# Hybrid edge passes of a four-layer GNN kernel: more strips and fewer gathered groups, the bias written into PSUM by ScalarE, two banks for expanded rows

## What is computed

```python
for l in range(5):
    h = leaky(x @ W1[l] + b1[l]) @ W2[l] + b2[l]                     # per node
    e = leaky(edge_attr @ We1[l] + be1[l]) @ We2[l] + be2[l]         # per edge, 32 -> 64 -> 64
    msg = h[src] * e * dot_scale[l]
    agg = segment_sum(msg, dst)
    out = x + agg * res_w[l]
    x = layer_norm(out) * ln_g[l] + ln_b[l]
```

## Time and profile before

| what | value |
|---|---|
| median of 3 runs | 14754.5 us (14753.59 to 14761.05) |
| the profiled execution, its own time | 14765.12 us |
| its span | 14763.1 us |
| PE busy | 11299.0 us, 77% of the span |
| POOL busy | 9919.2 us, 67% |
| DVE busy | 9782.0 us, 66% |
| ACT busy | 5832.6 us, 40% |
| mean granted TensorE clock | 0.860 of full speed |
| five hybrid passes, from their first gather to their last | 7346.8 to 13751.9 us |

### The profile page before, as it was taken

The page is one execution under the profiler, slowest core; times in us unless marked ns, Lnnn a source line. Parts: engine busy times, 40 slices in busy tenths (PEclk is TensorE's granted clock), DMA queues, the critical chain, the costliest instruction groups (busy, mean ns, idle before and its releaser), DMA issues. The chain is left out here.

```text
span 14763.1 us, 394431 instructions
## 1 busy us (share of the span) xinstructions
PE 11299.0 (77%) x124067; PEld 10168.6 (69%) x124067; DVE 9782.0 (66%) x18585; ACT 5832.6 (40%) x11169; POOL 9919.2 (67%) x10022
## 2 busy tenths in 40 slices
PE   0366666689566787878699979979997998899585
PEld 0244444588555787878588868868886887888485
DVE  8777777567798323232477777777777777777524
ACT  0000000122266555555355445544444554455354
POOL 0377777677496675757377767767776776777474
PEclk9877777555567999999899989999998999999798
DMA  3122222222177565656444434434443443444363
GB/s 115 33 56 56 56 56 56 56 78 80 58 247 252 186 201 161 201 166 198 112 130 131 120 91 131 131 78 134 131 127 86 131 130 86 129 131 130 107 203 116
DMA packets 1281251, 1800.75 MB, mean 122 GB/s; under 512 B 558054, under 2 KB 817510, under 8 KB 1279974
## 3 DMA queue, kind: packets, MB, share of 16 engines
q1 hardware_dynamic: 978113, 1423.30, 30.6%
q0 software_dynamic: 296960, 327.11, 10.0%
q10 hardware_dynamic: 5040, 35.13, 0.6%
HBM read 1475.83 MB, written 308.76 MB: 121 GB/s over the span
## 5 line engine op out<-in xcount | busy, mean ns | idle before, releaser
L1181 POOL DMA_INDIRECT rows_buf<-feature_table,idx_buf x4320 | 4529.1, 1048 | 1388.4 <-issue 1101.2
L881 POOL DMA_INDIRECT rows_buf<-feature_parts,idx_buf x2176 | 2058.9, 946 | 944.2 <-issue 362.8
L920 ACT ACTIVATE sums_space<-banks 128x384 bf16<-128x384 f32 x3920 | 1661.5, 450 | 1268.3 <-PE banks L937 1245.3
L937 PE MATMUL banks<-table_parts,tmp 128*128 128x192 bf16 x13720 | 1786.0, 247 | 372.9 <-DMA tmp<-one_hots 372.3
L735 POOL DMA_INDIRECT rows_buf<-attention_table,idx_buf x1664 | 1574.8, 946 | 554.2 <-issue 554.2
L1271 PE MATMUL banks<-attr_buf,params 128*128 128x256 f32 x5660 | 1587.6, 404 | 300.1 <-DMA attr_buf<-cell_attr 167.3
L950 PE MATMUL banks<-sums_space,tmp 128*128 128x192 bf16 x13720 | 1781.7, 247 | 0.0
L1233 ACT ACTIVATE sums_space<-onehot 128x448 bf16<-128x448 f32 (+1 forms) x1415 | 845.1, 597 | 2361.6 <-DVE onehot L1369 995.9
L1283 PEld LDWEIGHTS banks<-params,hidden 128*128 128x128 f32 x11320 | 1519.5, 195 | 195.1 <-issue 8.2
L1283 PE MATMUL banks<-params,hidden 128*128 128x128 f32 x11320 | 1521.7, 278 | 0.0
L937 PEld LDWEIGHTS banks<-table_parts,tmp 128*128 128x128 fp8e4 x13720 | 1196.0, 98 | 398.8 <-issue 396.5
(11 more groups left out here) (395 smaller groups left out, 20166.5 us busy)
## 6 DMA issues: line engine op xcount, KB each, us to landing
tmp<-one_hots SPq DMA_DIRECT2D x1855, 448.0 KB
attr_buf<-cell_attr SPq DMA_DIRECT2D x875, 128.0 KB
one_hots<-tmp SPq DMA_DIRECT2D x245, 448.0 KB
attr_buf<-attr SPq DMA_DIRECT2D x653, 128.0 KB, 2.2
rows_buf<-feature_table,idx_buf POOLq DMA_INDIRECT x4320
gathered_rows<-rows_buf SPq DMA_DIRECT2D x208, 272.0 KB, 2.1
rows_buf<-gathered_rows SPq DMA_DIRECT2D x208, 272.0 KB
rows_buf<-feature_parts,idx_buf POOLq DMA_INDIRECT x2176
```

The source lines that it names most:

```text
L881: pool.indirect_dma_start(out=far_rows[:, u, t, :], out_offset=None, in_=table3, in_offset=bass.IndirectOffsetOnAxis(ap=idx_buf[:, u, t:t ...
L920: act.activation(cell_rows[:, q, 0:width], bank[q][:, 0:width], ACT.Copy).then_inc(s_cells_sb, 1)
L937: ins = pe.matmul(bank[q][:, j % 2 * 3 * D:(j % 2 + 1) * 3 * D], src_cells[:, k, j, side * P:(side + 1) * P], table_parts[:, 2 * (k * CELL ...
L1181: pool.indirect_dma_start(out=edge_rows[:, u, t, :], out_offset=None, in_=table, in_offset=bass.IndirectOffsetOnAxis(ap=idx_buf[:, u, t:t ...
```

## The change

The split becomes 29 strips (203 near works) and 92 gathered groups: 295 works. The cycle is now 4 strips and 12 groups, 40 works, run 6 times, with a tail of 5 strips and 20 groups, 55 works. In the cycle each strip goes 0 F 1 2 F 3 4 F 5 6; in the tail the first goes 0 F 1 2 F 3 F 4 5 F 6, the other four 0 F 1 F 2 3 F 4 5 F 6.

ScalarE writes be2, repeated over 8 tiles, into the edge bank (`put_bias`, 128x512 f32), between `high_part` and `copy_hidden` in its turn; the bias product on PE and `split_bias` go. The expanded rows alternate between banks 0 and 7. Where a near work has no own edges (k of 2 and more), the last fp32 product of the second edge layer covers 64 columns rather than 128.

```diff
-        self.cell_strips, self.cell_rest, self.cell_turn = 25, 3, 8
-        self.cell_turns = (self.cell_strips - self.cell_rest) // 2
+        self.cell_strips, self.cell_cycle, self.cell_rest, self.cell_turn = 29, 4, 5, 12
+        self.cell_turns = (self.cell_strips - self.cell_rest) // self.cell_cycle
...
-        CYCLE, REST = mixed(2, L.cell_turn), mixed(L.cell_rest, L.cell_rest_far)
+        CYCLE, REST = mixed(L.cell_cycle, L.cell_turn), mixed(L.cell_rest, L.cell_rest_far)
...
-            expanded, far_bank, strip_bank = bank[0], bank[1], bank[6]
+            far_bank, strip_bank = bank[1], bank[6]
+
+            def expanded_bank(w):
+                return bank[7 * w.slot]
...
                 act.sem_inc(s_edge, 2)
-                act.sem_inc(s_row, 1)
+                act.sem_inc(s_row, 2)
...
+                def put_bias(w, early):
+                    if not early:
+                        act.wait_ge(s_mult, w.n - 1)
+                    act.activation(edge_bank(w).rearrange("p (t d) -> p t d", d=D), b2.unsqueeze(1).broadcast_to([P, G, D]),
+                                   ACT.Copy).then_inc(s_biased, 1)
...
                     if w_next:
                         high_part(w_next)
                     if w_ahead:
+                        put_bias(w_ahead, early)
                         copy_hidden(w_ahead)
                     if w_next:
                         middle_part(w_next)
...
-                def edge_features(w, early=False):
+                def edge_features(w):
                     pe.wait_ge(s_leaky, w.n + 1)
-                    if not early:
-                        pe.wait_ge(s_mult, w.n - 1)
-                    pe.matmul(edge_bank(w), ones_bf, bias_parts.unsqueeze(1).broadcast_to([P, G, D]), start=True, stop=False)
+                    pe.wait_ge(s_biased, w.n + 1)
                     for half in range(2):
                         for pair in range(2):
                             t, at = 4 * half + 2 * pair, (2 * pair + half) * P
-                            ins = pe.matmul(edge_bank(w)[:, t * D:(t + 2) * D], hidden[:, w.side, at:at + P], w2,
-                                            start=False, stop=(half == 1 and pair == 1))
+                            end = min(t + 2, CELLS if w.near and w.k >= 2 else G)
+                            ins = pe.matmul(edge_bank(w)[:, t * D:end * D], hidden[:, w.side, at:at + P], w2[:, 0:(end - t) * D],
+                                            start=False, stop=(half == 1 and pair == 1), skip_group_check=True)
...
                     if w.near:
-                        dve.wait_ge(s_row, w.chunk + 2)
+                        dve.wait_ge(s_row, w.chunk + 3)
...
-                dve.wait_ge(s_load, 16)
-                split_bias(dve, then)
                 split_rests(dve, stage)
```

More of the change, by code:

```diff
@@ L53, in __init__ @@
         self.slices = -(-self.groups // self.far_groups)
-        self.cell_strips, self.cell_rest, self.cell_turn = 25, 3, 8
-        self.cell_turns = (self.cell_strips - self.cell_rest) // 2
+        self.cell_strips, self.cell_cycle, self.cell_rest, self.cell_turn = 29, 4, 5, 12
+        self.cell_turns = (self.cell_strips - self.cell_rest) // self.cell_cycle
         self.cell_far = self.groups - self.cell_strips * (W // G)
         self.cell_rest_far = self.cell_far - self.cell_turns * self.cell_turn
-        assert self.cell_strips % 2 == self.cell_rest % 2 and 0 <= self.cell_rest_far < self.cell_rest * CHUNKS
+        assert self.cell_turns * self.cell_cycle + self.cell_rest == self.cell_strips and self.cell_cycle % 2 == 0
+        assert 0 <= self.cell_rest_far < self.cell_rest * CHUNKS
         assert self.cell_far % U == 0 and self.cell_turn % U == 0
@@ L369, in build @@
         s_taken = sem("s_taken")
+        s_biased = sem("s_biased")
         numbers = [s.num for s in semaphores]
@@ L1097, in work @@
                 c = h * CHUNKS + k
-                return Work(near=True, s=i * 2 + h, k=k, g=None, u=None, round=None, tiles=CELLS, slot=c % 2, attr=c % 2,
-                            loads=i * CHUNKS + (c // 2 + 1), chunk=i * 2 * CHUNKS + c, **common)
+                return Work(near=True, s=i * L.cell_cycle + h, k=k, g=None, u=None, round=None, tiles=CELLS, slot=c % 2, attr=c % 2,
+                            loads=i * (L.cell_cycle // 2 * CHUNKS) + (c // 2 + 1), chunk=i * (L.cell_cycle * CHUNKS) + c, **common)
             per = L.cell_turn
@@ L1113, in hybrid_pass @@
             w1, b1 = COLS["l2"](params, "We1"), COLS["l2"](params, "be1")
-            w2 = COLS["l2"](params, "We2")
+            w2, b2 = COLS["l2"](params, "We2"), COLS["l2"](params, "be2")
             @block.sync
@@ L1242, in copy_rows, with turn @@
                         act.wait_ge(s_mult, w.n - (0 if w.follows_near else 1))
-                    act.activation(cell_row[:, 0:CELLS, :].rearrange("p t d -> p (t d)"), expanded[:, 0:CELLS * D], ACT.Copy).then_inc(s_row, 1)
-                def turn(w_next, w_later, w_ahead):
+                    act.activation(cell_row[:, 0:CELLS, :].rearrange("p t d -> p (t d)"), expanded_bank(w)[:, 0:CELLS * D], ACT.Copy).then_inc(s_row, 1)
+                def turn(w_next, w_later, w_ahead, early=False):
                     if w_next:
@@ L1253, in turn @@
                         copy_rows(w_later)
-                turn(None, None, work(0, 0))
-                turn(None, work(0, 0), work(0, 1))
+                turn(None, None, work(0, 0), True)
+                turn(None, work(0, 0), work(0, 1), True)
                 turn(work(0, 0), work(0, 1), work(0, 2))
@@ L1325, in turn @@
                     if w_later:
-                        edge_features(w_later, early)
+                        edge_features(w_later)
                     if w:
@@ L2518, in build @@
         p2 = lambda name: COLS["l2"](params, name)
-        def split_bias(dve, then):
-            row, left, (high_row, middle_row) = p2("be2"), (far_total, strip_total[:, 0, :]), (sent[:, 0, 0, 0:D], sent[:, 0, 1, 0:D])
-            then(dve.tensor_copy(high_row, row))
-            then(dve.tensor_tensor(left[0], row, high_row, ALU.subtract))
-            then(dve.tensor_copy(middle_row, left[0]))
-            then(dve.tensor_tensor(left[0], left[0], middle_row, ALU.subtract))
-            then(dve.tensor_scalar(left[1], high_row, is_part[:, 0:1], None, ALU.mult))
-            then(dve.scalar_tensor_tensor(out=left[1], in0=middle_row, scalar=is_part[:, 1:2], in1=left[1], op0=ALU.mult, op1=ALU.add))
-            then(dve.scalar_tensor_tensor(out=bias_parts, in0=left[0], scalar=is_part[:, 2:3], in1=left[1], op0=ALU.mult, op1=ALU.add))
         with nc.Block() as block:
@@ L2612, in _ @@
                 first_window(dve, then, HF)
-                for n in range(3):
-                    then(dve.tensor_scalar(is_part[:, n:n + 1], iota_p[:, :], float(n), None, ALU.is_equal))
-                then(dve.memset(ones_bf, 1.0))
-                split_bias(dve, then)
         stage_end()
```

5 lines of the change are left out of this document (1 added, 4 removed).

## The result

The changed kernel takes 14670.93 us (median of 5 runs, 14667.18 to 14676.68). The kernel before, in 5 runs alongside, takes 14757.92 us. The ratio is 0.9942 [0.9929, 0.9956], so the change makes the kernel **0.6% faster, by 87 us**. The prediction was 14887 us, 0.9% slower: wrong in sign, and the range (from 14700) missed the time by 29 us.

The account below looks back on a forecast made before the run. PE was taken to bound the loop, gathers the tail. Six loop turns of 159.6, five ends of 4.0, tail 222 and start 8.3 gave 1208 us a pass against 1180.6; over five passes, less 5: 14887 us, range 14700 to 15000.

Parts of the forecast that it names:

- The limit moves from PE to the chain: In the loop, the back-and-forth between PE, ScalarE and VectorE sets the pace: 39.9 us a strip, above PE's 36.9.
- Near turns of 3.7 that wait for the hidden copy: VectorE's near turns without sums grow from 3.17 to 3.69 us and wait for ScalarE's hidden copy, no longer for PE.
- 0.53 for the bias: ScalarE's bias write between high part and hidden copy costs 0.53 us, the middle between 0.49 and 0.57.
- k=0 at 5.00, k=1 at 4.49: Loop turns with own edges: 2.53 and 2.02 us to the hidden copy without the bias, then 2.47 more.
- `leaky` to low part 0.68: Within a turn on VectorE, 0.68 us from `leaky` to the low part, a term of the 2.47 after the hidden copy's start.
- The two kinds that were to keep their length: Near turns with one-hot and sums stay at 3.86 us, far turns behind k=0 with the strip's sums at 3.89.
- A loop end 4.0: Each of 5 jumps back costs 4.0 us a pass: VectorE's standstill of 2.7 plus 1.3 for ScalarE.
- ScalarE's stop, 1.3 of up to 2.7: At a loop's end ScalarE, its body grown to 264 rows, also stops: between 0 and 2.7 us, taken as 1.3.
- The start, 8.3: The first loop turn of a pass takes 8.3 us more than its strips, kept from the kernel before.
- The tail, 222: The 55 works after the loop take 222 us a pass, 4.04 each, with gathers no longer a limit of their own.
- PE's clock: Rival: PE, busy for 90% of the loop, is granted 0.9, a strip takes 41 us on PE: 15050 us, chance 0.07.
- The first rival, 14480: Rival: the bias hides in ScalarE's idle time and turns keep their length, -54 us a pass, 14480 us, chance 0.15.

Follow-up runs that it names:

- the late bias: The changed kernel with ScalarE's bias write moved behind the last copy of its turn: 14449.95 us (0.9779 to the kernel before), on another chip 14440.45 (0.9777).

## Why the prediction was wrong, step by step

The mechanism was right and the sum was not: the step that failed is the size of the own-edge turns k=0 and k=1. A pass was forecast at 1208 us and took 1160.5. Of the 47.5 us between, the five later loop turns hold (163.6 - 158.7) x 5 = 24.5, the first one (159.6 + 8.3) - 160.3 = 7.6, and the tail 222 - 206.7 = 15.3.

- *The limit moves from PE to the chain*: right, by the waits above and by the late bias. *Near turns of 3.7 that wait for the hidden copy*: 3.63 in the middle of all of the loop, right. *Far 3.86*: 3.78. *0.53 for the bias*: 0.53. The Trainium skill (ScalarE: Activation LUTs, "Step-by-step: what each stage is for") would have led towards 0.49. It compares where ScalarE writes to, and so do the rows of one far turn above: the write into PSUM takes 0.59 us, 0.53 from start to start, the high part beside it, which goes to SBUF, 0.63 and 0.54. The advantage is small here, and part of it may be the other output type.
- *k=0 at 5.00, k=1 at 4.49*: **here the forecast failed.** They measure 4.25 and 4.09. In the prediction their hidden copies start 2.53 and 2.02 us after the multiply, without the bias. Both came from the earlier trace rows, one stretch that spans a loop's end, and there VectorE waits for instructions ahead of the own edges. The other k=0 of the same loop turn in the kernel before has 9072.59 - 9070.45 = 2.14, and over all turns the medians are 2.15 and 1.71. In the changed kernel the medians are 2.41 and 2.24 with the 0.53 in them. So what a loop's end adds to its own two turns was put into every strip: 0.38 of the 0.75 us that k=0 was off, and 0.31 of the 0.40 of k=1. Another 0.27 of k=0 (2.15 against 2.41 - 0.53) goes with own edges that now follow the multiply more closely, 8986.26 - 8985.56 = 0.70 us in one turn of the changed kernel, against 0.94 in the ordinary k=0 shown below; why is open. The own-edge turns hold 27.6 of the 47.5 us by the loops, and some 7 more by the tail.

The kernel before, DVE's and ACT's timelines, one ordinary k=0 and one at a loop's end:

```profile
9070.45 0.62 DVE L1366 TENSOR_TENSOR onehot<-banks,early 128x448 f32<-128x448 f32 x1 [0.86 <-PE banks L1283]
9071.39 0.55 DVE L1380 SCALAR_TENSOR_TENSOR early<-banks,far_ident,stage 128x64 f32<-128x64 f32 x2 [0.32 <-issue]
...
9114.06 0.62 DVE L1366 TENSOR_TENSOR onehot<-banks,early 128x448 f32<-128x448 f32 x1 [0.89 <-PE banks L1283]
9115.37 0.56 DVE L1380 SCALAR_TENSOR_TENSOR early<-banks,far_ident,stage 128x64 f32<-128x64 f32 x2 [0.69 <-issue]
```

```profile
9072.59 0.67 ACT L1228 ACTIVATE hidden<-banks,params 128x512 f32<-128x512 f32 x1
...
9116.58 0.67 ACT L1228 ACTIVATE hidden<-banks,params 128x512 f32<-128x512 f32 x1
```

- *`leaky` to low part 0.68*: 0.61 in a far turn (9004.82 - 9004.21) and in those with own edges. In a near turn without sums it took 0.65 (9007.87 to its low part). That is 0.03 to 0.07 us a turn, as much as the doubt of 0.04 that the prediction allowed for the bias. The two kinds that were to keep their length did: 3.85 for the 3.86, and 3.90 for the 3.89.
- Together a strip takes 4.25 + 3.90 + 4.09 + 2 x 3.85 + 2 x 3.78 + 3 x 3.63 = 38.4 us, not 39.9. Four of them save 6.0 us a loop turn.
- *A loop end 4.0*: 158.7 - 4 x 38.4 = 5.1, somewhat dearer. *ScalarE's stop, 1.3 of up to 2.7*: in the stretch of the earlier trace rows its waits on "issue" were 8.2 us in 3, and are 16.6 in 6 now, over five ends instead of nine or ten. Five of the six are loop ends, at 2.8 to 3.3 us each, so ScalarE does stop at every end with its body of 264 rows. VectorE's multiply comes 2.4 to 3.1 us late there, with a body of 520. The Trainium skill (Runtime: NRT & Kernel Launch, "Instruction fetch mechanics") has a stop where the jump's target lies outside the two blocks held, 512 instructions together. The prediction read this as no stop for any shorter body, and by that ScalarE's would be 0. The measurement decides against that reading. Which two blocks are held when a loop jumps back is in no row, so the page's own sentence is neither borne out nor refuted. The three waits of the kernel before, 2.7 us each, lie in the middle of loop turns.

The two rows, of before and of the change:

```profile
ACT sums_space L1233 <- issue: 8.2, 3, 2.7
```

```profile
ACT sums_space L1235 <- issue: 16.6, 6, 3.3
```

- *The start, 8.3*: 160.3 - 4 x 38.4 = 6.7, nearly right.
- *PE at 36.9 us a strip and 90% of the loop*: 0.946 x 158.7 / 4 = 37.5, so PE's work was nearly right, and its share is higher because the turn is shorter.
- *The tail, 222*: 206.7. A near turn takes 3.51 there and a far one 3.70, and k=0 with a group's sums 4.96, which had been put at 5.81 from the earlier trace rows. The gather limit goes, as forecast. Three turns of the tail of the changed kernel:

```profile
9653.37 0.68 DVE L1377 TENSOR_TENSOR onehot<-banks,rows_buf 128x512 f32<-128x512 f32 x1
9657.07 0.61 DVE L1374 TENSOR_TENSOR onehot<-banks,early 128x448 f32<-128x448 f32 x1
9660.58 0.62 DVE L1374 TENSOR_TENSOR onehot<-banks,early 128x448 f32<-128x448 f32 x1
9665.54 0.69 DVE L1377 TENSOR_TENSOR onehot<-banks,rows_buf 128x512 f32<-128x512 f32 x1
```

(The first is a far turn, 3.70; then near, 3.51; k=0 with the sums, 4.96.) That turns are 0.07 to 0.12 us shorter here than in the loop may be due to the loop's waits on registers; it wasn't tried.

- *Half-wide product at nothing*: right. *The second bank a gain on PE alone*: it measures 0.2% with the bias on PE. *POOL no limit*: right. *PE's clock*: 0.99 in the loop as before, so that rival is out. *split_bias at 5 us*: too small to be shown. Of the two profiled executions the changed one reaches its first multiply 18 us earlier (7331.6 against 7349.7), and another run of nearly the same kernel doesn't (7351), so stages that the change doesn't touch vary by more.
- *The first rival, 14480*, asked whether the near turn would keep 3.17. In the change it doesn't. With the write behind the copies it does (3.15), and the kernel takes 14450 and 14440. The rival's price was right for another place of the same instruction. The prediction saw that ScalarE's idle time "lies elsewhere", and that is where the bias has to be put.

How near the sign was: with the medians of before, k=0 would have been put at 2.15 + 2.47 = 4.62 and k=1 at 1.71 + 2.47 = 4.18, 0.7 less a strip, and with the right length between `leaky` and low part another 0.4. That is 1.1 x 24 = 26 us a pass, so the forecast would have been 1182 us, no change. The tail, 15 us shorter than forecast, makes most of the difference to 1160.5. The 27.4 us by which a pass was to grow are 0.9 us in each of its 29 strips, and the two own-edge turns of a strip alone were off by 0.75 + 0.40.

## What to carry to other kernels

An engine that is busy for half of the time has its idle time in particular places of its order. Between two links of a back-and-forth chain an instruction put on it costs up to its whole length: of the 0.53 us, 0.48 in a near turn without sums, 0.2 in a far one (3.78 against 3.58), and nothing where VectorE had its own work meanwhile. Behind the last link it cost nothing (3.15, where the kernel before has 3.17). So the place was worth 1.6% on the chips where the chain set the pace, more than the change itself. Read a turn's length as a middle over many turns of its kind, and never from one that holds a loop's end. When a change has two parts that feed different limits (here a gather-bound tail and a PE-bound loop), each alone can measure as nothing while both together gain.

## What the runs showed of the hardware

A ScalarE write of 128x512 into PSUM takes 0.592 us, 0.53 from start to start, the middle of the bounds of the earlier trace rows, about as long as the plain copy out of PSUM (0.60, 0.49). Of 64 columns it takes 0.209 us, 0.15 from start to start, on a slower chip:

```profile
L1240 ACT ACTIVATE banks<-params x1475: 587/592/607, 7321.0 to 13653.2; 128x512 f32<-128x512 f32 x185
```

At a loop's end PE too stands still, longer with the longer body. In the stretch 8753 to 9650 the expansion waited on "issue" for 25.0 us in 10 times (2.5 each) before, and for 21.1 us in 5 times (4.2 each) in the changed kernel:

```profile
PE banks L1295 <- issue: 25.0, 10, 2.6
```

```profile
PE banks L1303 <- issue: 21.1, 5, 4.9
```

And one and the same program took 14681 us on one chip and 18896 on another, with ScalarE's and VectorE's instructions of nearly equal length, more time between instructions, and a granted clock of 0.81 rather than 0.86. There the place of the bias made no difference, and that program gained 2.9% over the kernel before where it gained 0.6% on the other. So how much one version gains over another can depend on the chip.
